# Attention output projection as five split float32r products, with the split of o made from PSUM

## What is computed

```python
xw = windows of 8x8 tokens, C = 192, nh = 8 heads of hd = 24
h = _layernorm(xw, ln1_g, ln1_b)
qkv = (h @ qkv_w).reshape(-1, N, 3, nh, hd)
attn = jax.nn.softmax(jnp.einsum('bnhd,bmhd->bhnm', q, k) * scale, axis=-1)
o = jnp.einsum('bhnm,bmhd->bnhd', attn, v).reshape(-1, N, C)
a = o @ proj_w + proj_b + xw
```

## Time and profile before

| | us |
|---|---|
| median of 3 runs | 3452.77 |
| lowest, highest | 3448.55, 3457.2 |
| the profiled execution, its own time | 3452.14 |
| its span, first to last instruction | 3450.4 |
| mean granted TensorE clock | 0.982 of full speed |
| attention stage, first product of step 3 to last residual sum | 24.87 to 887.86 |

### The profile page before, as it was taken

How to read it: one execution, slowest core, us unless ns; L and a number is a source line. 1 busy time by engine, 2 the same in 40 slices (tenths; PEclk the granted TensorE clock), 3 DMA queues, 4 the chain that set the end, 5 groups by cost and what they waited for, 6 DMA issues and landing times. The chain is left out here.

```text
span 3450.4 us, 86941 instructions
## 1 busy us (share of the span) xinstructions
PE 3299.2 (96%) x31288; PEld 3199.6 (93%) x31288; DVE 2625.2 (76%) x6465; ACT 2016.5 (58%) x5410; POOL 1149.2 (33%) x2151
## 2 busy tenths in 40 slices
PE   7999999999799999999978869999999899999999
PEld 6999998899799999999978869989999899989999
DVE  6777777777467676767679989979999788875554
ACT  5777777777344444444436656668999655532222
POOL 4333333333244444444323300014444356630000
PEclk9999999999899999999989989999999999999999
DMA  2677888711012111212178866645555788877775
GB/s 67 183 237 237 259 283 271 254 56 46 22 50 55 48 53 48 56 44 56 48 201 258 265 186 186 199 130 161 169 166 165 211 235 234 236 223 231 226 223 175
DMA packets 473215, 556.40 MB, mean 161 GB/s; under 512 B 78805, under 2 KB 332122, under 8 KB 472794
## 3 DMA queue, kind: packets, MB, share of 16 engines
q1 hardware_dynamic: 447450, 531.57, 51.7%
q10 hardware_dynamic: 25344, 19.27, 1.7%
HBM read 405.31 MB, written 258.67 MB: 192 GB/s over the span
## 5 line engine op out<-in xcount | busy, mean ns | idle before, releaser
L1468 PE MATMUL PS<-dw_grid,dw_mats 128*128 128x196 f32 (+1 forms) x3840 | 627.3, 327 | 34.2 <-DVE dw_mats L1400 34.2
L1468 PEld LDWEIGHTS PS<-dw_grid,dw_mats 128*128 128x128 f32 x3840 | 626.5, 192 | 34.6 <-issue 34.6
L1283 PE MATMUL PS<-mlp_w,mlp_hid 128*128 128x192 f32 x2352 | 414.4, 326 | 0.5 <-ACT mlp_hid L820 0.5
L1396 DVE COPY dw_grid<-X 32x392 f32<-32x392 f32 (+1 forms) x480 | 290.0, 604 | 163.8 <-PE PS L1468 149.6
L1283 PEld LDWEIGHTS PS<-mlp_w,mlp_hid 128*128 128x128 f32 x2352 | 378.6, 190 | 0.8 <-ACT mlp_hid L820 0.8
L1823 PE MATMUL PS<-grn_gain,down_hi 128*128 128x384 f32 x1176 | 353.2, 362 | 10.3 <-POOL X_low L1776 10.3
L820 ACT ACTIVATE mlp_hid<-PS,mlp_b 128x256 f32<-128x256 f32 x588 | 247.5, 472 | 112.1 <-PE PS L811 112.1
L546 ACT ACTIVATE att_vbd<-PS,att_rs 64x96 f32<-64x96 f32 x784 | 264.7, 338 | 12.7 <-DVE att_rows L476 5.4
L1776 POOL TENSOR_TENSOR X_low<-X,down_hi 128x128 fp32r<-128x128 f32 x196 | 208.9, 1066 | 152.5 <-ACT down_hi L1786 152.5
L1134 POOL COPY X<-mlp_x 128x192 f32<-128x192 f32 x196 | 114.7, 585 | 432.5 <-DVE mlp_x L1210 432.0
L1435 ACT ACTIVATE dw_res<-PS,dw_brow 128x196 f32<-128x196 f32 x192 | 81.8, 426 | 298.2 <-PE PS L1468 298.2
(11 more groups left out here) (254 smaller groups left out, 9805.2 us busy)
## 6 DMA issues: line engine op xcount, KB each, us to landing
scratch_hid<-hid_hid SPq DMA_DIRECT2D x196, 320.0 KB, 3.4
down_hid<-scratch_hid SPq DMA_DIRECT2D x196, 320.0 KB, 3.6
scratch_wide<-scratch_taps SPq DMA_DIRECT2D x64, 960.0 KB, 6.1
dw_raw<-scratch_wide SPq DMA_DIRECT2D x96, 640.0 KB, 4.3
scratch_wide<-scratch_taps SPq DMA_DIRECT2D x64, 768.0 KB, 5.5
dw_raw<-scratch_wide SPq DMA_DIRECT2D x96, 512.0 KB, 3.6
scratch_u<-mlp_u SPq DMA_DIRECT2D x56, 378.0 KB, 3.0
att_x<-in_x SPq DMA_DIRECT2D x196, 96.0 KB, 2.3
```

The costliest lines, as they stand in the source:

```text
L1283: last = nc.tensor.matmul(psD[i], hid[:, p.buf(2), m, i * 128:(i + 1) * 128], w2[:, m, :], start=(m == 0), stop=(m == MC - 1))
L1396: last = nc.vector.tensor_copy(dst, src)
L1468: last = nc.tensor.matmul(dst[:, :, ys, :], m, src, start=(i == 0), stop=(i == len(steps) - 1))
```

## The change

The projection becomes five float32r products of 192 columns. o and the weights are each split in a high part (float32r) and a low part. The first 128 channels take three products (high by high, high by low, low by high). The last 64 channels are transposed twice, so that one product with `wpb` (rows 0 to 63 the high weights, 64 to 127 the low ones) takes two terms; the fifth product takes their low part, and in rows 64 and 96 of `wpr` the high and low part of the bias, met by ones in `ol`.

In each step: GpSimd copies 64 columns of o (`twice`, signals `o_twice`), for which its body now runs at every step, with `columns` at even ones and `spread` at odd ones; the transposes wait for `o_twice` and for `o_split` of the block before; ScalarE writes `oh` (one buffer) from psOT after the projection of the block before; VectorE forms `ol` (one buffer) in two subtractions from psOT, placed ahead of the residual sum; the projection waits for `o_split`; and the scores wait for `o_split` where they waited for `ot_ready`. The ring of xt has 2 places for 3. The weights' split moves to `projection()`, on VectorE at the end of step 4.

```diff
-    XR, TR = 12, 3
+    XR, TR = 12, 2
...
-    wp = s.sb("wp", [128, KC, C])
+    wpa = s.parts("wpa", [128, C])
+    wpb = s.sb("wpb", [128, C], F32R)
+    wpr = s.sb("wpr", [128, C], F32R)
...
-    o = s.sb("o", [128, 2, C])
-    ot = s.sb("ot", [128, 2, KC, 128])
-    room = X[:, 120:130, :].rearrange("p b c -> p (b c)")
+    o = s.sb("o", [128, 2, 256])
+    oh = s.sb("oh", [128, 256], F32R)
+    ol = s.sb("ol", [128, 256], F32R)
...
-    LOADS = 3 + 6 + 1 + 1
+    LOADS = 3 + 6 + 3 + 2
...
-            sp.dma_start(wp[0:CH, :, :], a["L0_conv_proj_w"].rearrange("(k p) n -> p k n", k=KC)).then_inc(wloaded, 16)
-            sp.dma_start(pbrow[96:97, :], a["L0_conv_proj_b"].partition_broadcast(1)).then_inc(wloaded, 16)
+            for at_, rows_, k in ((slice(0, 128), slice(0, 128), 0), (slice(0, 64), slice(128, C), 1), (slice(64, 128), slice(128, C), 1)):
+                sp.dma_start(wp[at_, k, :], a["L0_conv_proj_w"][rows_, :]).then_inc(wloaded, 16)
+            for r in (64, 96):
+                sp.dma_start(pbrow[r:r + 1, :], a["L0_conv_proj_b"].partition_broadcast(1)).then_inc(wloaded, 16)
...
+            def twice(b):
+                pool.wait_ge(q["o_ready"], b.n + 1)
+                nc.gpsimd.tensor_copy(o[:, b.buf(2), C:256], o[:, b.buf(2), 128:C]).then_inc(q["o_twice"], 1)
...
+            def body(t):
+                b = t.back(AHEAD + 3)
+                if b.inside(NB):
+                    twice(b)
+                if t.inside(NB) and t.j % 2 == 0:
+                    columns(t.pair())
+                if t.inside(NB) and t.j % 2 == 1:
+                    spread(t)
+            unrolled(NB, LAG, body)
...
-                dve.wait_ge(q["pbias"], 1)
-                nc.vector.tensor_tensor(wp[96:97, 0, :], psPB, pbrow[96:97, :], ALU.add).then_inc(q["weights"], 1)
-                dve.wait_ge(q["weights"], 1)
                 dve.wait_ge(q["split"], 2)
+
+            def projection():
+                for i, r in enumerate((64, 96)):
+                    dve.wait_ge(q["pbias"], 1)
+                    nc.vector.tensor_tensor(pbrow[r:r + 1, :], psPB[i], pbrow[r:r + 1, :], ALU.add).then_inc(q["pb"], 1)
+                nc.vector.tensor_copy(wpa[0][:, :], wp[:, 0, :]).then_inc(q["pw"], 1)
+                nc.vector.tensor_copy(wpb[:, :], wp[:, 1, :]).then_inc(q["pw"], 1)
+                nc.vector.tensor_copy(wpr[0:64, :], wp[0:64, 1, :]).then_inc(q["pw"], 1)
+                nc.vector.tensor_copy(wpr[64:128, :], zeros[64:128, :]).then_inc(q["pw"], 1)
+                nc.vector.tensor_copy(ol[64:128, 128:256], zeros[64:128, 0:128]).then_inc(q["pw"], 1)
+                dve.wait_ge(q["pw"], 5)
+                dve.wait_ge(q["pb"], 2)
+                nc.vector.tensor_tensor(wpa[1][:, :], wp[:, 0, :], as_f32(wpa[0][:, :]), ALU.subtract).then_inc(q["weights"], 1)
+                nc.vector.tensor_tensor(wpb[64:128, :], wp[64:128, 1, :], as_f32(wpb[64:128, :]), ALU.subtract).then_inc(q["weights"], 1)
+                nc.vector.tensor_copy(wpr[64:65, :], pbrow[64:65, :]).then_inc(q["weights"], 1)
+                nc.vector.tensor_copy(wpr[96:97, :], pbrow[96:97, :]).then_inc(q["pb_high"], 1)
+                for r in (64, 96):
+                    nc.vector.tensor_scalar(ol[r:r + 1, 128:256], zeros[r:r + 1, 0:128], 0.0, 1.0, ALU.mult, ALU.add).then_inc(q["ones"], 1)
+                dve.wait_ge(q["pb_high"], 1)
+                nc.vector.tensor_tensor(wpr[96:97, :], pbrow[96:97, :], as_f32(wpr[96:97, :]), ALU.subtract).then_inc(q["weights"], 1)
...
+                b = t.back(AHEAD + 4)
+                if b.inside(NB):
+                    dve.wait_ge(q["ot_ready"], b.n + 1)
+                    if b.reached(1):
+                        dve.wait_ge(q["proj"], b.n)
+                    nc.vector.tensor_tensor(ol[:, 0:128], psOT[:, 0:128], as_f32(oh[:, 0:128]), ALU.subtract)
+                    nc.vector.tensor_tensor(ol[0:64, 128:256], psOT[0:64, 128:256], as_f32(oh[0:64, 128:256]), ALU.subtract).then_inc(q["o_split"], 1)
                 b = t.back(AHEAD + 5)
...
                     act.wait_ge(q["ot"], b.n + 1)
-                    if b.reached(2):
-                        act.wait_ge(q["proj"], b.n - 1)
-                    nc.scalar.activation(ot[0:CH, b.buf(2), :, :], psOT.rearrange("p (k n) -> p k n", k=KC), ACT.Identity).then_inc(q["ot_ready"], 1)
+                    if b.reached(1):
+                        act.wait_ge(q["proj"], b.n)
+                    nc.scalar.activation(oh[:, :], psOT, ACT.Identity).then_inc(q["ot_ready"], 1)
...
                 b = t.back(AHEAD + 4)
                 if b.inside(NB):
-                    pe.wait_ge(q["o_ready"], b.n + 1)
+                    pe.wait_ge(q["o_twice"], b.n + 1)
                     pe.wait_ge(q["shifted"], b.upto(3))
                     if b.reached(1):
-                        pe.wait_ge(q["ot_ready"], b.n)
-                    for k in range(KC):
-                        last = nc.tensor.transpose(psOT[:, k * 128:(k + 1) * 128], o[:, b.buf(2), k * CH:(k + 1) * CH], ident[:, :])
-                    last.then_inc(q["ot"], 1)
+                        pe.wait_ge(q["o_split"], b.n)
+                    nc.tensor.transpose(psOT[:, 0:128], o[:, b.buf(2), 0:128], ident[:, :])
+                    nc.tensor.transpose(psOT[:, 128:256], o[:, b.buf(2), 128:256], ident[:, :]).then_inc(q["ot"], 1)
                 b = t.back(AHEAD + 5)
                 if b.inside(NB):
-                    pe.wait_ge(q["ot_ready"], b.n + 1)
+                    pe.wait_ge(q["o_split"], b.n + 1)
                     pe.wait_ge(q["shifted"], b.upto(4))
                     if b.reached(1):
                         pe.wait_ge(q["resid"], b.n)
-                    nc.tensor.matmul(psPJ, ot[0:CH + 1, b.buf(2), 0, :], wp[0:CH + 1, 0, :], start=True, stop=False)
-                    nc.tensor.matmul(psPJ, ot[0:CH, b.buf(2), 1, :], wp[0:CH, 1, :], start=False, stop=True).then_inc(q["proj"], 1)
+                    else:
+                        pe.wait_ge(q["weights"], 5)
+                        pe.wait_ge(q["ones"], 2)
+                    terms = ((oh[:, 0:128], wpa[0][:, :]), (oh[:, 0:128], wpa[1][:, :]), (ol[:, 0:128], wpa[0][:, :]), (oh[:, 128:256], wpb[:, :]),
+                             (ol[0:97, 128:256], wpr[0:97, :]))
+                    for j, (h, w) in enumerate(terms):
+                        last = nc.tensor.matmul(psPJ, h, w, start=(j == 0), stop=(j == 4))
+                    last.then_inc(q["proj"], 1)
...
                     if b.reached(3):
-                        pe.wait_ge(q["ot_ready"], b.n - 2)
+                        pe.wait_ge(q["o_split"], b.n - 2)
```

More of the change, by code:

```diff
@@ L324, in attention @@
     pbrow = room[:, 2 * W + 384:2 * W + 384 + C]
+    wp = room[:, 2 * W + 384 + C:2 * W + 384 + 3 * C].rearrange("p (k n) -> p k n", k=KC)
+    zeros = room[:, 2 * W + 384 + 3 * C:2 * W + 384 + 4 * C]
     psS = PS[:, 0:4, 0:128]
     psPJ = PS[:, 1, 128:128 + C]
-    psOT = PS[0:CH, 2, 128:384]
+    psOT = PS[:, 2, 128:384]
     psPT = PS[:, 4, :]
@@ L335, in attention @@
     psMean = [PS[:, i, 0:HALF] for i in range(2)]
-    psVB = PS[0:CH, 7, 0:KC]
-    psPB = PS[96:97, 4, 0:C]
+    psVB = PS[:, 7, 0:KC]
+    psPB = [PS[r:r + 1, 4, 0:C] for r in (64, 96)]
     wloaded, ready, loaded, tloaded = s.sem("wloaded"), s.sem("ready"), s.sems("loaded", 4), s.sems("tloaded", TR)
@@ L341, in attention @@
              "stats", "aggr", "var_ok", "rstd", "h_high", "h_low", "h_ready", "half_a", "half_b", "a_kept", "b_kept", "v_ready",
-             "turned", "qk_ready", "scores", "max", "shifted", "probs", "pt", "pt_ready", "pv", "recip", "o_ready", "ot", "ot_ready",
+             "turned", "qk_ready", "scores", "max", "shifted", "probs", "pt", "pt_ready", "pv", "recip", "o_ready", "ot", "ot_ready", "o_split", "o_twice", "pb", "pb_high", "pw", "ones",
              "proj", "resid")
     q = {x: s.sem(x) for x in names}
-    LOADS = 3 + 6 + 1 + 1
+    LOADS = 3 + 6 + 3 + 2
     READY = 6 + 4 * 2
@@ L394, in _ @@
             pool.wait_ge(ready, 4)
-            nc.gpsimd.memset(ot[96:97, :, 0, :], 1.0).then_inc(ready, 1)
+            nc.gpsimd.memset(zeros, 0.0).then_inc(ready, 1)
             pool.wait_ge(ready, 5)
@@ L401, in _, with columns @@
             pool.wait_ge(ready, 6)
[L403 to L406, removed]
+            def twice(b):
+                pool.wait_ge(q["o_ready"], b.n + 1)
+                nc.gpsimd.tensor_copy(o[:, b.buf(2), C:256], o[:, b.buf(2), 128:C]).then_inc(q["o_twice"], 1)
+            def columns(u):
                 if u.n == 3:
@@ L514, in body @@
                                             view(mx[:, b.buf(2), :], [[2, 4], [1, 2], [0, 64]]), ALU.subtract).then_inc(q["shifted"], 1)
+                if t.n == 4:
+                    projection()
                 if t.n == 12:
@@ L564, in _ @@
             pe.wait_ge(q["wide"], 1)
-            for k in range(KC):
-                m = slice(QK + k * CH, QK + k * CH + CH)
```

(15 more changed lines are left out.)

12 lines of the change are left out of this document (7 added, 5 removed).

## The result

The kernel after takes 3596.23 us (median of 4 runs, 3592.72 to 3603.24) against 3454.98 us for the kernel before on the same chip: a ratio of 1.0416, 95% interval 1.0396 to 1.0436. That is slower, by 141 us. The forecast was 3610, range 3560 to 3668. The profiled execution took 3597.42 us, its span is 3595.6 us.

The account below looks back on a forecast made before the run. TensorE set the pace before; after the change a chain through ScalarE and VectorE would make the step 5.05 us for 4.26. Profiled 3452.1 + 152 + 6.5 = 3610.6, forecast 3610 us, range 3560 to 3668.

Parts of the forecast that it names:

- the chain: Attention step: last projection product, `oh`, two subtractions, residual sum, then scores; 5.05 us a step for 4.26.
- The added wait: TensorE ahead of the scores, for `o_split` and `resid`: stands 0.82 us a step; +0.79 over 192 steps, 152 us.
- TensorE's own work: Five float32r products replacing four float32 instructions in the projection: saves 0.03 us a step, 6 us in 196.
- The good end of that bound: TensorE's projection without the extra 0.09 us for the first float32r product: saves 0.12 us a step.
- The subtractions: VectorE's two for `ol`, ahead of the residual sum: 0.20 us each; by the Trainium skill some 0.25.
- Once only: Outside the repeated steps: DMA issues +1.7, bias sum -0.4, `projection()` +2.8, last four steps +2.4; together +6.5 us.
- the tail: Last four attention steps, without scores: the chain gains two subtractions, +2.4 us.
- kept its clock: Rival 3: idle TensorE drops to the lower clock level; 4270 us if for good; 3%.
- VectorE's total: Rival 2: VectorE's in-order waits stretch its 3.76 us and bind; steps about 4.45, 3495 us; 3%.
- The fourth: Rival: residual sum of t-8 not behind the subtractions, 0.2 to 0.3 us a step less, 3560; in forecast's low end.
- The first rival: Attention waits met in time, TensorE stays the bound: 3430 to 3452 us; 5%, another 3% within 0.3%.
- the bounds of a step: Added time per attention step: low 0.56 us, high 1.18, giving 3566 to 3686 us.

Follow-up runs that it names:

- the fourth kernel: Kernel after, with the transposes of queries and keys and of the probabilities moved ahead of the scores in TensorE's list: 3540.50 us, ratio 1.0259.

## Why the prediction was right

**The bound moved from TensorE's list to the chain**, as put. The added wait stands at 192 steps, as many as forecast, and takes 153 us in all. Its length, piece by piece, predicted and measured in the step shown: scores to next first product 1.27 and 1.26; ten products 1.42 and 1.41; transposes and projection up to its last product 0.76 and 0.64; its end 0.27 and 0.27; `oh` released after 0.04 and 0.10; `oh` to `ol` 0.41 and 0.42; two subtractions 0.40 and 0.40; residual sum 0.36 and 0.34; release of the scores 0.12 and 0.15. Sum 5.05 and 4.99. The sum is a little closer than its terms: the terms that came out shorter make 0.16, the longer ones 0.10. Doubling `oh` took 0.40 out of it, and added work on it came through at 0.41 a step.

**TensorE's own work** was mis-sized, on the safe side: from the transposes of o to the products with the values it is 0.85 for 0.96, 0.11 saved where I said 0.03. Transposes and the first product together took 0.31 (407.10 to 407.41), not 0.43; from the last product to the products with the values it is 0.21, not 0.17. The good end of that bound was right. What was saved up to the last product lies in the chain as well: it is the 0.64 for 0.76 above, the largest miss of a term.

**The subtractions.** They followed each other after 0.21 and 0.19 us. By "Perfetto Trace Analysis" of the Trainium skill, section "Optimizing Scalar/DVE Operations", with its 125 ns of overhead on PSUM, I had estimated 0.25 each. These rows do not agree with it for this use: beyond 128 columns at 1 ns, 0.06 to 0.08 is left.

**Number of steps and their mean.** 0.79 a step and 192 steps made 152; 0.729 a step over 195 made 142. The difference is mainly the 0.06 above: both kernels have a mean 0.07 to 0.08 above their local step, as the forecast assumed when it took only differences. Most of the 14 us between forecast and median is in this term. **Once only** 6.5 was forecast, 7.0 came: the first copy of the weights 9.54 for 8.36 (+1.2, forecast +1.7), `projection()` from 35.62 to 39.45 (3.8, forecast 3), the tail +2.3 (forecast +2.4).

**The rivals.** TensorE busy at 85% kept its clock: the window above shows 1.00. VectorE's total did not bind: extra work off the chain cost 3 us. The fourth, that the sum were not behind the subtractions, was given 3560; the kernel that makes it so took 3570, and 3559 with the waits in the right order. The first rival, that all waits are met in time, failed by a factor of two: from the start of the last projection product at 407.74 the cover lasts 0.82 us (to 407.95 + 0.61), the chain 1.53 (to the end of the residual sum at 409.27). The prediction set 1.6 against its 0.78 there, which includes the release of the scores; up to the end of the sum its own terms give 1.48.

**Slips in the prediction's arithmetic.** The terms it names for the bounds of a step give 0.59 and 1.22, not 0.56 and 1.18; the measured 0.73 lies inside either. Its chances add up to 103%. The lower end of its range, 3560, is not cut off the bounds but below their low end of 3566.

**What the forecast did not see** did not touch its number: that the banks also bind the other way, and that the place of a small product in TensorE's list has a price, which the kernel after pays as often as the kernel before. Both broke the expectation of the fourth kernel.

## What to carry to other kernels

When a step gets a new producer in the middle, write down the loop through every shared buffer and bank, with one buffer counted as a wait for the last reader, and compare it with the bound engine's list; here cheaper products for TensorE could not pay for 1.53 us of chain with 0.82 us of cover. Try extra work on and off the suspected chain: 84 us against 3 decides at once. And before groups are moved in TensorE's list, look for the idle time ahead of small products: keep small ones together, and put the wait that ends last at the end of a row of waits.

## What the runs showed of the hardware

- Behind full weights (128 rows and columns) the first small product (64 columns, or 24 rows, of weights) started 0.09 us later than the usual distance: 0.25, 0.21 and 0.20 us behind a float32 projection, a float32r projection and transposes. The weight loads stood still for 0.23, 0.10 and 0.17 meanwhile. Four transposes took 0.05 longer behind small products. One more such pair of changes cost the kernel before 0.125 us a step and 0.63% of its time. Whether it is the shape of the weights or the number of moving columns that counts, no run separates.
- TensorE went on 0.15 us after VectorE's end when the wait met last stood last, and 0.26 when one more, long met, stood behind it.
- Five float32r products of 192 columns, 0.11 apart, with two transposes ahead of them took less than four float32 instructions with theirs: 0.85 for 0.96 us.
